# Decay exponents of a state-space scan: a TensorE product of bf16 parts replaced by one GpSimd difference and ScalarE's Relu

## The reference, cut to what matters

```
dA = dt * A                                   # A = -exp(A_log), so dA is negative
A_cum = cumsum(dA)                            # within a chunk
Lmat = exp(A_cum[l] - A_cum[s])   for l >= s, else 0
Y_diag = einsum(C[l], B[s], Lmat[l, s], x_dt[s])
states = einsum(B, exp(A_cum[last] - A_cum), x_dt)
new_state = state * exp(A_cum[last]) + states
Y_off = einsum(C, state, exp(A_cum))
y = Y_diag + Y_off + D * x ;  g = y * silu(z) ;  out = rmsnorm(g) @ W_out.T
```

## Time and profile before

| | |
|---|---|
| median of 3 runs | 3621.58 us (3617.08 to 3626.28) |
| time of the profiled execution | 3622.66 us |
| its span, first to last instruction | 3620.7 us (1.96 us lie around it) |
| scan's 128 steps | about 1663 to 3210 us of the span |
| busy in the span | PE 95%, DVE 74%, ACT 54%, POOL 25% |
| mean granted TensorE clock | 0.976 |

### The profile page before, as it was taken

How to read it: one execution, slowest core, us unless ns; L and a number is a source line. 1 busy time by engine, 2 the same in 40 slices (tenths; PEclk the granted TensorE clock), 3 DMA queues, 4 the chain that set the end, 5 groups by cost and what they waited for, 6 DMA issues and landing times. The chain is left out here.

```text
span 3620.7 us, 58447 instructions
## 1 busy us (share of the span) xinstructions
PE 3422.7 (95%) x20912; PEld 2392.3 (66%) x20912; DVE 2696.8 (74%) x5252; ACT 1947.7 (54%) x2496; POOL 918.3 (25%) x821
## 2 busy tenths in 40 slices
PE   8889999999999788969999999999999999979998
PEld 6544444444444467756777777777777777758886
DVE  3577777777777384677999889998998889864444
ACT  3156656666667633434666566665666666543332
POOL 0022222222222200003443434443444444420000
PEclk9989999999999898989999999999999999989999
DMA  7443443443432211236555655565555555530100
GB/s 231 72 91 93 106 89 89 112 89 104 101 88 89 97 36 35 84 133 201 183 175 180 222 174 164 177 217 184 182 177 192 189 179 177 177 131 27 35 12 24
DMA packets 254975, 463.04 MB, mean 128 GB/s; under 512 B 48224, under 2 KB 62432, under 8 KB 251616
## 3 DMA queue, kind: packets, MB, share of 16 engines
q1 hardware_dynamic: 254688, 459.30, 41.6%
HBM read 363.49 MB, written 95.16 MB: 127 GB/s over the span
## 5 line engine op out<-in xcount | busy, mean ns | idle before, releaser
L510 ACT ACTIVATE probs<-prob_scores 128x1024 f32<-128x1024 f32 (+3 forms) x640 | 572.4, 896 | 381.0 <-PE prob_scores L440 373.1
L460 PE MATMUL times_v<-probs,VS 128*64 128x256 f32 (+2 forms) x4608 | 612.4, 382 | 14.2 <-ACT outT L537 13.0
L557 DVE TENSOR_REDUCE part_max<-ring 128x1 f32<-128x512 f32 x720 | 462.8, 685 | 115.3 <-PE ring L432 113.6
L49 PE MATMUL sc_pip<-sc_xh,sc_wl 128*128 128x512 f32 x1024 | 453.1, 443 | 18.6 <-DMA sc_xl<-x_low 14.0
L460 PEld LDWEIGHTS times_v<-probs,VS 128*64 128x64 f32 x4608 | 279.7, 136 | 253.7 <-issue 162.6
L1627 POOL TENSOR_TENSOR sc_xdd<-sc_xdt,sc_small 128x512 f32<-128x512 f32 x128 | 248.2, 1939 | 640.7 <-DVE sc_xdt L1849 640.7
L51 PE MATMUL sc_pip<-sc_xh,sc_wh 128*128 128x512 f32 x1024 | 405.8, 396 | 0.0
L50 PE MATMUL sc_pip<-sc_xl,sc_wh 128*128 128x512 f32 x1024 | 402.4, 393 | 0.0
L1840 DVE SCALAR_TENSOR_TENSOR sc_ca<-sc_xr,sc_chan,sc_ca 128x512 f32<-128x512 f32 x384 | 292.9, 763 | 13.6
L440 PE MATMUL prob_scores<-QS,KS 50*128 50x512 f32 (+3 forms) x1280 | 298.7, 463 | 1.6 <-ACT probs L510 1.6
L440 PEld LDWEIGHTS prob_scores<-QS,KS 50*128 50x128 f32 x1280 | 119.6, 184 | 214.2 <-ACT probs L510 121.0
(11 more groups left out here) (333 smaller groups left out, 7215.2 us busy)
## 6 DMA issues: line engine op xcount, KB each, us to landing
sc_wh<-scan_W_high SPq DMA_DIRECT2D x256, 256.0 KB, 2.7
sc_wl<-scan_W_low SPq DMA_DIRECT2D x256, 256.0 KB, 3.0
sc_ce<-scan_expa SPq DMA_DIRECT2D x128, 512.0 KB, 5.2
sc_woh<-scan_Wo_high SPq DMA_DIRECT2D x128, 256.0 KB, 4.0
sc_wol<-scan_Wo_low SPq DMA_DIRECT2D x128, 256.0 KB, 4.6
w_raw<-in_Wg SPq DMA_DIRECT2D x64, 256.0 KB, 2.8
scan_W_high<-w_hi SPq DMA_DIRECT2D x64, 256.0 KB, 2.0
scan_W_low<-w_lo SPq DMA_DIRECT2D x64, 256.0 KB, 2.3
```

The costliest lines, as they stand in the source:

```text
L49: pe.matmul(out, ll, rh, start=start, stop=False)
L460: mm = pe.matmul(po[MV * s:MV * (s + 1), CHUNK - w + n * h:CHUNK - w + (n + 1) * h], VS[p % 2][:, j, :], PT[u % NPT][:, s, n * h:(n + 1) * ...
L510: act.activation(PT[u % NPT][:, :, 0:w], pb[u % 2][:, :, 0:w], ACT.Exp).then_inc(exped, 1)
L557: dve.tensor_reduce(to, slot(n)[:, 0:w], AX.X, ALU.max).then_inc(emptied, 1)
```

## The change

The expert stage no longer splits the running sums. ScalarE copies them in f32 (`ex_asum`), SP writes them to `scan_acum` (8 DMAs, as for `scan_expa`), and TensorE transposes them into a fourth kind of the table `scan_small`, so that each position has its own sum in its own partition. In the scan SP loads, for each step, the row of sums of the 8 heads into all 128 partitions (`sc_later`, 512 KB, two buffers). GpSimd subtracts it from the position's own sum, which is repeated over 128 columns, and writes `sc_M` directly (`exponents`, semaphore `apart`); ScalarE takes Relu in place. The product and its PSUM tile are gone, and so are `sc_arhs`, `sc_alhs`, their memsets and the three `affine_select` at the scan's start.

```diff
 # scan, GpSimd
+                def exponents(t):
+                    b, c = t // QT, t % QT
+                    pool.wait_ge(later_in[t % 2], 16 * (t // 2 + 1))
+                    pool.wait_ge(small_in[b % 2], 16 * (b // 2 + 1))
+                    if t >= 2:
+                        pool.wait_ge(y_prod, t - 1)
+                    pool.tensor_tensor(M[t % 2][:, :, :], small[b % 2][:, c, 3, :].unsqueeze(2).to_broadcast([P, GH, CL]),
+                                       later[t % 2][:, :, :], ALU.subtract).then_inc(apart, 1)
...
                     pool.tensor_tensor(heads(sd[:, :]), heads(st[:, grp, :]), bc(t, 2), ALU.mult).then_inc(s_decayed, 1)
                     if t + 1 < STEPS:
+                        exponents(t + 1)
                         decay_inputs(t + 1)
 # scan, TensorE
-                def exponents(t):
-                    c = t % QT
-                    pe.wait_ge(sums_in[c], 64 * (t // QT + 1))
-                    if t:
-                        pe.wait_ge(relued, t)
-                    for h in range(0, GH, 4):
-                        mm = pe.matmul(p_arg[:, h:h + 4, :], alhs[:, c * CL:(c + 1) * CL], arhs[:, c, h:h + 4, :], start=True, stop=True)
-                    mm.then_inc(arg, 1)
...
                     if t + 1 < STEPS:
-                        exponents(t + 1)
                         turn_x(t + 1)
 # scan, ScalarE
-                    act.wait_ge(arg, t + 1)
-                    if t >= 2:
-                        act.wait_ge(y_prod, t - 1)
-                    act.activation(M[t % 2][:, :, :], p_arg[:, :, :], ACT.Relu, scale=-1.0).then_inc(relued, 1)
+                    act.wait_ge(apart, t + 1)
+                    act.activation(M[t % 2][:, :, :], M[t % 2][:, :, :], ACT.Relu).then_inc(relued, 1)
 # scan, SP
+                def load_later(t):
+                    src = D["acum"][group_of(t) * TT + chunk_of(t)].partition_broadcast(P)
+                    sp.dma_start(later[t % 2][:, :, :].rearrange("p h l -> p (h l)"), src).then_inc(later_in[t % 2], 16)
...
-                    if t + 5 < STEPS:
-                        sp.wait_ge(arg, t + 2)
-                        load_sums(t + 5)
+                    if t + 3 < STEPS:
+                        sp.wait_ge(apart, t + 2)
+                        load_later(t + 3)
 # expert stage, SP
+                        for made_by, name, src, out in ((asum_made, "acum", asum, asum_out), (ea_made, "expa", ea, ea_out)):
...
-                        for n, a in enumerate((a1, a2, a3)):
-                            sp.dma_start(D["sums"][n][:, chunk(c)], a[:, :]).then_inc(sums_out, 16)
```

More of the change, by code:

```diff
@@ L993, in experts @@
         z, dA = carve([P, QT, NH]), carve([P, QT, NH])
-        u, sq, s2 = (carve([P, QT * NH]) for n in range(3))
+        u, sq = (carve([P, QT * NH]) for n in range(2))
+        s2 = sb("ex_s2", [P, QT * NH])
         sm = carve([P, GROUPS, QT, KINDS, GH])
         upto, after, ones = (carve([P, P]) for n in range(3))
-        a1, a2, a3 = (sb(f"ex_a{i}", [NH, CHUNK], BF16) for i in range(3))
+        asum = sb("ex_asum", [NH, CHUNK])
         rest, ea = carve([NH, CHUNK]), carve([NH, CHUNK])
@@ L1076, in _ @@
                     if part == 2:
+                        for made_by, name, src, out in ((asum_made, "acum", asum, asum_out), (ea_made, "expa", ea, ea_out)):
+                            sp.wait_ge(made_by, c + 1)
+                            for grp in range(GROUPS):
+                                sp.dma_start(D[name][grp * TT + QT * c:grp * TT + QT * (c + 1), :].rearrange("c (h l) -> h c l", l=CL),
+                                             src[grp * GH:(grp + 1) * GH, :].rearrange("h (c l) -> h c l", l=CL)).then_inc(out, 16)
+                    if part == 3:
                         sp.wait_ge(sm_copied, c + 1)
                         sp.wait_ge(sm_exped, 2 * c + 2)
+                        sp.wait_ge(sm_turned, c + 1)
                         sp.dma_start(D["small"][:, :, QT * c:QT * (c + 1), :, :], sm[:, :, :, :, :]).then_inc(small_out, 16)
[L1080 to L1084, removed]
-                        for n, a in enumerate((a1, a2, a3)):
-                            sp.dma_start(D["sums"][n][:, chunk(c)], a[:, :]).then_inc(sums_out, 16)
-                    if part == 3:
                         sp.wait_ge(bc_silu, c + 1)
@@ L1188, in scan_part @@
                     if part == 3:
+                        await_bank(c, "turn")
+                        pe.wait_ge(asum_made, c + 1)
+                        for r in range(QT):
+                            mm = pe.transpose(bank(c, "turn")[:, r * NH:(r + 1) * NH], asum[:, r * P:(r + 1) * P], g.ident[0:NH, 0:NH])
+                        mm.then_inc(asum_turned, 1)
                         pe.wait_ge(bc_silu, c + 1)
@@ L1472, in scan @@
         woh, wol = sb("sc_woh", [P, NWO, E], F32R), sb("sc_wol", [P, NWO, E], F32R)
-        arhs, alhs = sb("sc_arhs", [P, QT, GH, CL], BF16), sb("sc_alhs", [P, CHUNK], BF16)
+        later = [sb(f"sc_later{b}", [P, GH, CL]) for b in range(2)]
         small = [sb(f"sc_small{b}", [P, QT, KINDS, GH]) for b in range(2)]
@@ L1554, in _ @@
                 load_small(0)
+                for t in range(2):
+                    load_later(t)
                 for t in range(NE):
@@ L1558, in _ @@
                     load_bc(t)
-                for n in range(2):
-                    sp.wait_ge(ip, n + 1)
-                    load_w(n + NW)
-                sp.wait_ge(setup, N_SETUP)
-                for t in range(QT):
-                    load_sums(t)
-                for n in range(2, PER):
+                for n in range(PER):
                     sp.wait_ge(ip, n + 1)
@@ L1582, in _ @@
                             sp.wait_ge(s_decayed, t)
+                            sp.wait_ge(apart, t)
                         load_small(b + 1)
@@ L1627, in decay_inputs @@
                     pool.tensor_tensor(xdd[t % 2][:, :, :], xdt[t % 2][:, :, :], bc(t, 1), ALU.mult).then_inc(xdd_made, 1)
-                pool.wait_ge(cleared, 4)
-                for n in range(3):
-                    if n:
-                        pool.wait_ge(setup, n)
-                    pool.affine_select(out=arhs[0:AK, :, :, :], in_=arhs[0:AK, :, :, :], compare_op=ALU.not_equal, fill=-1.0,
-                                       base=-3 - GH * n, pattern=[[0, QT], [-1, GH], [0, CL]],
-                                       channel_multiplier=1).then_inc(setup, 1)
+                def exponents(t):
[6 more added lines that the diff above has]
+                                       later[t % 2][:, :, :], ALU.subtract).then_inc(apart, 1)
+                exponents(0)
+                pool.wait_ge(cleared, 2)
                 decay_inputs(0)
```

61 lines of the change are left out of this document (23 added, 38 removed).

## The result

The changed kernel takes **3706.61 us** in the median of 4 runs (3702.03 to 3711.56); the kernel before, run beside it, takes 3622.86 us (3617.08 to 3626.28). The ratio is 1.0233, with a 95% interval of 1.0216 to 1.0249. The forecast was 3717 us, in a range of 3655 to 3785. The profiled execution took 3703.92 us, with a span of 3702.0 us.

What follows compares the result with a forecast made beforehand. The prediction took TensorE to bound the scan, with DVE out of room in two of four steps. Its terms, 83 + 6 + 4 + 2 = +95 us on the profiled 3622.7, gave 3717.7, predicted as 3717 us, range 3655 to 3785.

Steps and rivals of the forecast that it cites:

- TensorE's 0.44 us a step: Scan: TensorE loses two products a step, 56 us in all; a block would take 46.8 us if PE stayed the bound.
- The subtraction at 2.0 us: Scan, GpSimd: the new 1024-column subtraction each step takes 2.0 us, estimated between 1.9 and 2.4.
- Rival 2: Scan: the subtraction runs at 2.4 us, +1.2 a block, 3756 us, or 3797 with full low clock; 25 in 100.
- DVE stands for 1.9 us in a convolution step: Scan, two convolution steps a block: DVE is held 1.9 us in each while GpSimd's subtraction runs.
- Rival 3: Scan: softer lock or missed idle time, DVE pays 1.3 us twice, nothing on `sc_ce`; 3663 us; 16 in 100.
- A block's path of 50.3 us, and 0.3 for the later decays: Scan block, transposes to last Silu: 46.4 us becomes 50.3; waits behind the later Relu add 0.3 (0 to 1).
- 0.6 us a block for the lower clock: Scan: PE runs at 1.2 GHz for a while behind waits, costing 0.6 us a block, between nothing and 2.2.
- 32 blocks at +2.6 make +83: Scan: each block takes 51.2 us against 48.6, +2.6 us; over 32 blocks +83.
- group 7 +6, the last steps +4: Scan: subtraction hits `sc_ce` in group 7, 1.5 us in 4 blocks; last four steps lack projection cover, +1 each.
- Expert stage +2: Expert stage: eight more DMAs for three fewer, removed DVE splitting had cover; 0 to +3 us, taken as +2.
- Rival 1: Scan: PE stays the bound, 3566 us, if DVE pays under about 0.4 us each convolution step; 6 in 100.
- rival 4: Scan: a load becomes the bound, weight tiles 0.5 us late, +1 us a block on top, 3750 us; 5 in 100.

Runs made afterwards that it cites:

- product_too: Changed kernel plus two useless TensorE products of zeros a step, where the removed ones stood: 3693.68 us, ratio 1.0198.
- alone: Kernel before plus one GpSimd subtraction of 128x1024 a step on a buffer nobody reads, TensorE's product kept: 3665.43 us, ratio 1.0115.
- turn_act: Changed kernel with the expert stage's copy of the turned sums made by ScalarE in place of VectorE: 3699.90 us, ratio 1.0201.
- sums_direct: Changed kernel with the expert stage's sums by step made by one product in part 2, copied by ScalarE, without transposes: 3705.26 us, ratio 1.0235.
- relu_bias_last: Changed kernel with eight biased ScalarE Relus a step replacing GpSimd's subtraction, and turned sums last in the expert stage's bank rotation: 3583.46 us, ratio 0.9894.
- half_sub: Changed kernel with GpSimd's subtraction over four of the eight heads only: 3598.24 us, ratio 0.9938.
- no_pool: Changed kernel without GpSimd's subtraction, ScalarE's Relu reading the loaded sums directly: 3586.18 us, ratio 0.9896.
- lock_only: Changed kernel with Relu reading the loaded sums and GpSimd's subtraction writing a buffer nobody reads: 3692.37 us, ratio 1.0198.

## Why the prediction was right, point by point

The mechanism, the sign and the order of size were right. Two terms of the sum were mis-sized, one too high by 25 us and one too low by 11 to 13, so that the total was off by only 10 us; that it came so near is luck.

- **TensorE's 0.44 us a step.** Forecast: 56 us, and 46.8 us for a block that PE bounds. Measured without GpSimd: 52.0 us and 46.9 us.
- **The subtraction at 2.0 us, between 1.9 and 2.4.** The rows have 1.89 in the median and 1.96 in the mean. Rival 2 (2.4 us) is out.
- **DVE stands for 1.9 us in a convolution step.** The row has a copy of 1.82 us in place of 0.17, so 1.65 more, twice a block. The forecast named the second instruction of a convolution, and the `tensor_scalar` behind it in its reasoning; it was the copy ahead of that (in the last quarter the `tensor_scalar` itself). Rival 3, a softer lock, is out. On `sc_ce` I took 0.5 us a block and it was 52.5 / 32 = 1.6 in the mean (about 1.5 us more in one or both of a block's steps without convolution), of which part fell on idle time.
- **A block's path of 50.3 us, and 0.3 for the later decays.** product_too shows it at full clock: 50.77 us a block. alone, with the early decays, has 50.47 us between its borders (2311.49 to 2361.96), which is the 0.3. The sum of the path held, but not each of its terms: the convolution steps gave 3.3 us and not 3.8, `sc_ce` more than 0.5, and the 0.4 that I took off for the missing product gave nothing, since the changed kernel's full-clock blocks last 50.76 us without the product and product_too's 50.77 with it.

```profile
2311.49 0.66 PE L1685 MATMUL sc_pxt<-ident,sc_xT 128*128 128x128 f32 x4 [1.62 <-ACT sc_xT L1776]
...
2361.96 0.66 PE L1685 MATMUL sc_pxt<-ident,sc_xT 128*128 128x128 f32 x4 [1.62 <-ACT sc_xT L1776]
```

- **0.6 us a block for the lower clock (0 to 2.2).** Two neighbouring blocks of the changed kernel have 51.73 and 50.76 us, 51.2 in the mean, 0.5 above product_too's 50.77. Over the scan the difference is 11.2 us (0.35 a block): the lower clock cost 1.0 us and more in 11 blocks and nothing in most others. The first two blocks, where PE's work counts, took 0.7 us off, so this is rather a lower bound.
- **32 blocks at +2.6 make +83, group 7 +6, the last steps +4: the terms that failed.** These 93 us measured 68.0. Border to border against the kernel before, the 15 blocks of groups 2 to 6 in the first three quarters of the scan took 2.5 us more in the mean, as foretold. The rest did not: the first two blocks took 0.6 and 0.4 us more; those of the same groups in the last quarter, which have no history copy, 1.9; the three blocks of group 7 that lie between two borders 2.4, 1.1 and 2.0, where I had 4.1 (the first is 52.83 us against 50.39, from 1995.51 to 2045.90 us, the kernel before), and the ones right behind these 3.0; and the last block less than 1 us, where I had 2.6 + 1.5 + 4 = 8.1. That block projects and convolves nothing for a next one, so the 3.8 us of its two convolution steps were never there, and I had multiplied by 32 all the same. The +1.5 for group 7 was never tested by a run; its blocks show no such extra.
- **Expert stage +2 (0 to +3), scan's start 0.** Together they measured +13 to +15 us, outside the bounds I gave. The failed step is the one that ends in "the removed splitting on DVE had cover": I counted instructions and DMAs and missed that the new transposes enter the rotation of two banks, so that the next product but one waits for their copy. I read no wait of PE in that stage, nor that TensorE's clock falls behind such a wait, as the window 1500 to 1520 has it. turn_act and sums_direct, which were to take that wait away, moved or shortened it and did not clearly win the time back, and relu_bias_last won a part of it, so the cause of the whole +13 to +15 us stays open; the small transfers, which I did count, may hold a part, and no run separates them.
- **The sum.** +95 forecast, about +84 measured: 25 us too much in the scan, 11 to 13 too little ahead of it.
- **Rival 1 (TensorE stays the bound, 3566 us)** needed DVE to pay less than 0.4 us twice a block. half_sub shows this rival's world: with 1.1 us in place of 1.96 the scan is nearly PE's. For a subtraction half as long it was the right case; for this one it is out.
- **The signs.** Right: DVE at 95%, PE's waits on Silus (74.0 us, foretold as some 90), stretches of lower clock. No wait for a DMA or for the Relu took their place; rival 4 is out by no_pool. A slip in rival 2: with the low clock's full 2.2 us its time is 3756 + 1.6 x 32 = 3807 us and not 3797; the range doesn't hang on it.

In one line the scan's +68.0 us are: −52.0 for the product (no_pool against before), +108.3 for GpSimd's subtraction beside DVE (lock_only against no_pool; this holds the cost of the lower clock, some 11 us by product_too), +11.7 for decays that come later (changed against lock_only). Each is the difference of two runs, and they hold in this order of steps only: with the product in place the subtraction costs 40.4.

## What to carry to other kernels

Before work goes to an idle GpSimd, look at what VectorE does at that moment: it may pay for the whole length of the instruction, a three-element copy as much as a large one, and up to VectorE's slack it is free (1.12 us a step cost 11 us of the scan, 1.96 us cost 120). Work that fits ScalarE's form func(scale · x + bias), even cut into eight pieces of 0.39 us, was nearly free here (1489.5 us of scan against 1487.8 without it). Count a cost a block only over the blocks that have the instructions it falls on. And when buffers rotate, a new user of the ring moves all the others' waits: check who empties the bank that each product takes.

## What was unexpected of the hardware

Taking work from TensorE slowed the kernel where TensorE was not the bound: with 0.44 us a step less it idled longer at block borders, its mean granted clock in the scan fell from 1.00 to 0.97, and the run was 13 us slower than the same kernel with useless products. A GpSimd fill, which reads nothing, holds up VectorE's copies and `tensor_scalar` (633 and 802 ns in the mean with it, 490 and 552 without) but not its instructions with two SBUF inputs. And a Relu of 128x128 took 389 ns on ScalarE with a bias from SBUF, where I had expected 0.27 us from its copies of that size.
